# Handing ring room to GpSimd two tiles at a time, at twice the interval

## The reference, cut to what matters

```python
def _ref(z, edge_index, Wg, Ws, bg, W1, b1, W2, b2, W3, b3):
    src, dst = edge_index[0], edge_index[1]        # 200,000 edges, dst sorted
    msgs = z[src]                                  # a gather of rows
    agg = segment_sum(msgs, dst, 12500)
    deg = segment_sum(ones, dst, 12500)
    agg = agg / maximum(deg, 1.0)[:, None]
    h = relu(agg @ Wg + z @ Ws + bg)               # 128 -> 128
    h = tanh(h @ W1 + b1)                          # 128 -> 512
    h = tanh(h @ W2 + b2)                          # 512 -> 512
    return h @ W3 + b3                             # 512 -> 128

h = maximum(layernorm(x), 0.0)                     # x: 12500 x 128
out = x + _ref(h, stack([src, dst]), ...)
```

## Time and profile before

| what | value |
|---|---|
| median of 3 runs | 1659.8 us (1656.84 to 1665.99) |
| the profiled execution, its own time | 1658.69 us |
| its span, first to last instruction | 1656.8 us |
| PE busy | 1257.9 us (76%) |
| VectorE (DVE) busy | 956.5 us (58%) |
| POOL busy | 897.7 us (54%) |
| ACT busy | 552.8 us (33%) |

### The profile page before, as it was taken

One profiled execution on the slowest core, in us unless ns is written; L12 is line 12 of the kernel. 1 busy time (PEld: TensorE's weight loads), 2 busy tenths in 40 slices (PEclk: granted clock), 3 DMA queues, 4 the chain that ended last, 5 costly groups with the idle time before them and its releaser, 6 DMA issues.

```text
span 1656.8 us, 26502 instructions
## 1 busy us (share of the span) xinstructions
PE 1257.9 (76%) x9082; PEld 924.4 (56%) x9082; DVE 956.5 (58%) x1850; ACT 552.8 (33%) x1159; POOL 897.7 (54%) x953
## 2 busy tenths in 40 slices
PE   0204988778887888877888788888887888887888
PEld 0202656556665656565655555666555656565667
DVE  8806985546555575646556574547555665546441
ACT  6303441414142341414142341424142432324152
POOL 4473165656555655656566554656555554565530
PEclk9557999999989999888999999999988889899999
DMA  9611224142413314141414313141313313141410
GB/s 244 190 51 62 79 62 100 49 99 64 87 42 100 94 44 99 45 99 41 104 49 100 92 46 93 47 102 44 103 45 101 91 45 94 47 102 43 101 41 10
DMA packets 92829, 130.44 MB, mean 79 GB/s; under 512 B 47451, under 2 KB 73393, under 8 KB 88993
## 3 DMA queue, kind: packets, MB, share of 16 engines
q1 hardware_dynamic: 63773, 69.42, 16.3%
q0 software_dynamic: 28928, 59.30, 14.4%
HBM read 109.14 MB, written 13.09 MB: 74 GB/s over the span
## 4 chain that ended last, share of the span: by engine, by line
PE 54%; another core or an unknown queue 18%; issue 12%; ACT 8%; DVE 6%; DMA 1%; DVEq 0%; SPq 0%; ACTq 0%
PE banks L870 16%; PE banks L816 14%; PE banks L741 7%; PE banks L832 5%; PE banks L853 4%; PE banks L887 4%; DVE arena L1584 3%; ACT arena L1204 2%; ACT dense L1187 2%; ACT arena L1125 1%; PE banks L844 1%; PE banks L847 1%; ACT dense L1194 1%; PE banks L789 1%
## 5 line engine op out<-in xcount | busy, mean ns | idle before, releaser
L669 POOL DMA_INDIRECT ring<-h_table,idx_all x904 | 875.6, 969 | 670.3 <-issue 235.7
L870 PE MATMUL banks<-dense,w 128*128 128x256 f32 (+1 forms) x1568 | 430.5, 392 | 30.1 <-ACT dense L1194 16.8
L816 PE MATMUL banks<-xin,arena 128*128 128x256 f16 x2058 | 313.5, 287 | 103.9 <-issue 61.3
L1204 ACT CAST arena<-banks 128x512 f16<-128x512 f32 (+1 forms) x525 | 291.7, 579 | 206.2 <-PE banks L816 129.8
L870 PEld LDWEIGHTS banks<-dense,w 128*128 128x128 f32 x1568 | 272.2, 197 | 76.7 <-ACT dense L1194 20.8
L816 PEld LDWEIGHTS banks<-xin,arena 128*128 128x128 f16 x2058 | 190.3, 102 | 217.8 <-issue 117.4
L741 PE MATMUL banks<-ring,onehot 128*128 (+1 forms) x1008 | 194.6, 290 | 23.9 <-issue 18.1
L1574 DVE TENSOR_SCALAR arena<-arena,code_ptr 128x768 f16<-128x768 f16 (+1 forms) x336 | 133.6, 456 | 119.0 <-PE banks L816 89.6
L1584 DVE TENSOR_TENSOR arena<-node,banks 128x768 f16<-128x768 f16 (+1 forms) x168 | 152.5, 965 | 45.9 <-remote 24.7
L1194 ACT ACTIVATE dense<-banks,b2c 128x256 f32<-128x256 f32 (+1 forms) x196 | 92.0, 475 | 243.5 <-PE banks L870 125.7
L832 PE MATMUL banks<-arena 64*128 64x257 f16 x2058 | 146.5, 288 | 27.1 <-issue 21.5
(11 more groups left out here) (121 smaller groups left out, 871.2 us busy)
## 6 DMA issues: line engine op xcount, KB each, us to landing
arena<-unit_codes SPq DMA_DIRECT2D x21, 1568.0 KB
ring<-h_table,idx_all POOLq DMA_INDIRECT x904
xblk<-in_x_dram SPq DMA_DIRECT2D x48, 128.0 KB
out_dram<-dense SPq DMA_DIRECT2D x48, 128.0 KB
xin<-in_x_dram SPq DMA_DIRECT2D x4, 1232.0 KB, 17.0
h_table<-xin SPq DMA_DIRECT2D x4, 1232.0 KB
own_pair<-h_table SPq DMA_TRANSPOSE x98
w<-in_L_gnn_W_dram SPq DMA_DIRECT2D x1, 1024.0 KB
```

Source lines behind the costliest of these rows:

```text
L669: nc.gpsimd.indirect_dma_start(out=ring_tiles[:, t % RING, 0:2 * D], out_offset=None, in_=table, in_offset=bass.IndirectOffsetOnAxis(ap=id ...
L816: mm = nc.tensor.matmul(to, wide_l[:, piece % WSLOTS, k, j, :], tab[:, row_of(g, j), :], start=(j == 0), stop=(j == 1))
L870: mm = nc.tensor.matmul(l3_ps[c][:, 0:w], w2[:, q, c * P:(c + 1) * P], h2T[:, q, 0:w], start=(q == 0), stop=(q == HC - 1))
L1204: nc.scalar.copy(unit_msgs[:, 2 * pr:2 * pr + wide_of, 0:2 * D], unit_ps[pr % 2][:, 0:wide_of * 2 * D].rearrange("p (g d) -> p g d", d=2 * ...
```

## The change

Three numbers change. A lot is two tiles in place of one, the interval that `pace` keeps between lots is 2000 ns of its clock in place of 1000, and the opening has 24 lots free in place of 48, which are the same 48 tiles.

```diff
-LOT = 1
-OPEN_LOTS = 48
-LOT_NS = 1000
+LOT = 2
+OPEN_LOTS = 24
+LOT_NS = 2000
```

## The result

The changed kernel takes 1749.4 us (median of 4, 1736.2 to 1756.4), the kernel before 1659.9. The ratio is 1.056, with a 95% interval of 1.051 to 1.062. That is slower, as forecast, but by 90 us and not by 21, and outside the range, which ended at 1702. The profiled execution took 1736.2 us, the shortest of the four; what follows divides the 77 us between it and the profiled execution of before.

A forecast was written before the change was run, and what follows sets the result against it. It took PE's long hand-written order to bound the kernel, its time being PE's work plus gaps. Gathers, signals and late tiles at 0 and density at +21 us on 1659.8 gave 1681 us, range 1653 to 1702 (8 in 10).

The forecast's parts named there:

- Gathers: POOL's 904 gathers keep number, size and order, so POOL's work stays: 0 us.
- signals: 428 fewer raisings of `lot_free` on PE: taken as 0 us, with 13 us the upper bound of a gain.
- late tiles: PE's wait for tiles at seven tight steps behind extra blocks: 0 us; as a rival, 1672 us, chance 0.03.
- Density costs PE time: Gathers in denser runs leave PE idle more: 3% at up to two in 6 us, 44% at five.
- No change: Rival: each gather costs PE the same wherever it stands, or PE's density causes both; 1660 us, chance 0.21.
- faster: Rival: longer pauses between POOL's pairs of gathers let PE catch up; 1648 us, chance 0.14.
- The sum of +21 us: PE's added idle time from denser gathers, about two thirds of +33 us kept; forecast's chance 0.48.
- the +33 us before the cut: PE's idle time weighted with the new rule's gather shares: 283 us against 250, taken as an upper value.
- counts over 8 to 10 us: Rival slower by more: longer counts of gathers give PE +30 to +60 us, plus lower clock; 1705 us, chance 0.14.
- The lower clock: More gaps lower PE's granted clock: an eighth more would cost some 7 us, left to the range.
- The discount for a common cause: PE's fast stretches may give many lots and end in own gaps; about two thirds of +33 us kept.

The follow-up runs named there:

- 4: Changed kernel with each lot's second tile raised on its own at the next possible matmul, 856 raisings again: 1.001 of the kernel before, quick chip only.
- 1: Kernel before with only the first 64 tiles gathered: 1284.0 us against 1654.1 (0.776) on a slow chip, 1232.6 against 1271.4 (0.969) on a quick one.
- 2: Kernel before with LOT_NS = 1, a tile given as soon as the ring has room: 2093.7 us against 1654.1, ratio 1.261, slow chip.
- 6: Kernel before with a 128x256 memset on POOL behind every gather: 1560.9 us against 1639.5 (0.951), slow chip; the changed kernel with it: 0.972.
- the repetition: The changed kernel run again, unaltered, against the kernel before on a slow chip: 1742.1 us against 1654.1, ratio 1.051.
- 3: Pairs alone: kernel before, every second raising left out, POOL waiting once for two tiles: 1.011 of the kernel before on a slow chip, 1.004 quick.
- the short rows: Kernel before, gathers from the 65th tile fetching 128 bytes a row in place of 512: 0.999 and 1.000, quick chips only.
- the plain transfer: Kernel before, POOL issuing a plain transfer of 128 neighbouring rows in place of each gather from the 65th tile: 1242.3 us, 0.972, quick chip only.
- a smaller slowing: Kernel before with a 128x64 memset on POOL behind every gather: 1303.7 us, ratio 1.022, quick chip only.

## Why the prediction was wrong

The direction was right, and the mechanism on the chips of the result's kind; the size was off by a factor of four.

- *Gathers, signals, late tiles at 0 us*: right. 904 gathers at a median of 944 ns; no wait for tiles on a slow chip; 428 raisings make no measurable difference on a quick chip (4), though that alone was never tested on a slow one. The Trainium skill (TensorE: Matmul & The Clock Gate, The cost: per-tile semaphore tail) has some 26 ns for an increment, by which 428 fewer would save an estimated 11 us. That is not seen: on a quick chip the changed kernel, with 428 fewer than the kernel before, is at 1.001 (0.999 to 1.003), and 11 us would be 0.9%.
- *Density costs PE time*: right on slow chips, shown by experiments 1, 2 and 6. "No change" and "faster" fall there. On a quick chip the same density costs next to nothing, which nothing in the prediction allowed for. The rule of the Trainium skill (SBUF — State Buffer, Who interferes with whom) that transfers never contend with a compute engine agrees with the quick chips' runs (0.05 us a gather) and disagrees with the slow chips' (0.44 us a gather, at 74 GB/s in the mean).
- *The sum of +21 us for this term* is the step that failed. It measured +48 us of idle PE in the result's trace and +41 in that of the repetition; even the +33 us before the cut fall short. I had weighted a table of PE's idle share, by gathers in the 6 us before, with the shares of time that the new rule would give, and then cut it by a third because a stalling PE thins out the gathers. The shares moved less than the rule laid over the trace had said: five gathers in 6 us for 17% of the time, from 14%, where I had 21%. With the table of before, these shares would give no more idle time per us than before. What moved is the table: after the change the share is 0.49 at five gathers, 0.25 at four and 0.08 at two, where it was 0.44, 0.22 and 0.04. So 6 us is too short a memory for the link: reports come up to 53 us late (1) and 28 us late (2), when a run of gathers lasts that long. After the change 14 gathers behind 205 us stand ninth or later in their run, before only one. That count is not the whole link either, since the pairs alone (3) have 11 such gathers and cost 1.1%. I had counts over 8 to 10 us in hand, with +30 to +60 us, and gave them 14%.
- *The lower clock left to the range* was the second mistake: +28 us of PE's busy time (+44 in the repetition), where I had named 7. The matmuls behind a gap that brought the clock down to 1.2 GHz take longer, so a term in gaps has a second term in clock, here more than half as large. I had both in the earlier trace rows, where 11.30 us in place of 4.50 holds 7.41 us of busy PE, 2.9 more than in the fast case, and added only the gaps.
- *The discount for a common cause* ("a fast stretch of PE that gives many lots and ends in a gap of its own") was not needed: without gathers these gaps vanish (19 us of idle PE in place of 257).

What stays open: why some chips are slow in this way and others not; what in a gather holds PE's results up there (bytes, row transfers, the indirect form, completions), since the short rows and the plain transfer met quick chips alone; and how the price depends on the gathers over longer times. One rival has no run at all, that the recording of the trace has a part in it. Where reports are late, records of updates are missing too: 747 of the 856 raisings of `lot_free` in the trace of before, 853 without gathers on a slow chip.

## What to carry to other kernels

When an engine has gaps that no wait explains, count the work of every other engine around them, and run the kernel once without that work: it is the one experiment that gives the whole price, here 370 us that no view had a name for. Then compare the time of a semaphore's update with the end of the instruction that raised it, engine by engine. On a chip where this is so, a pace that spreads background transfers can be worth more than the work it adds, the opening burst included, and coarser grains of it cost twice, as gaps and as a lower clock. And time such a kernel on more than one chip: this change costs 5% on one and nothing on another, and a slower POOL gained 5% on the first kind, while a smaller slowing lost 2% on the second (neither of the two ran on the other kind).

## What the hardware showed that I had not expected

The kernel before differs by a factor of 1.30 between chips (1654 and 1272 us), and without gathers by 1.04 (1284 and 1233 us), all of it in one report that came 53 us late behind the opening run of gathers. In the cycle shown in experiment 2, eighteen gathers at 1.25 us bring PE from 11.4 to 5.0 of 12 us busy, and the first eight of them do nothing visible to its busy time. No run tests a kernel that spreads the opening gathers alone. No version with the right output was shown to beat both kernels on every chip; on a slow one the kernel before with the memset did, at 0.951.
